# Two expert layers with attention on one core: what GpSimd does between its last scatter-add and the end of the program

## The reference, cut to what matters

```python
x = x + xattn0(layernorm(x), ctx, ctx, mask, wq, wk, wv, wo)   # 16 heads
x = x + ffn0(layernorm(x), ...)                                # 8 experts, top 2, capacity 560
x = x + xattn1(layernorm(x), ctx, ctx, mask)                   # one head, no projections
x = x + ffn1(layernorm(x), gate_w, w1, w2, w3)                 # 8 experts, top 2, no capacity
```

## Time and profile before

| what | value |
|---|---|
| device time, median of 3 runs | 1093.72 us (1085.96 to 1093.96) |
| the profiled execution's own device time | 1096.15 us |
| its span, first to last instruction of the program | 1094.3 us |
| device time outside the span | 1.85 us |
| PE busy | 953.3 us, 87% of the span |
| DVE busy | 685.4 us, 63% |
| ACT busy | 544.7 us, 50% |
| POOL busy | 479.0 us, 44% |
| end of the last instruction that counts as work (POOL, L1545) | 1080.81 us |

### The profile page before, as it was taken

The page is one execution under the profiler, slowest core; times in us unless marked ns, Lnnn a source line. Parts: engine busy times, 40 slices in busy tenths (PEclk is TensorE's granted clock), DMA queues, the critical chain, the costliest instruction groups (busy, mean ns, idle before and its releaser), DMA issues.

```text
span 1094.3 us, 23134 instructions
## 1 busy us (share of the span) xinstructions
PE 953.3 (87%) x8011; PEld 876.2 (80%) x8011; DVE 685.4 (63%) x1937; ACT 544.7 (50%) x1212; POOL 479.0 (44%) x478
## 2 busy tenths in 40 slices
PE   5899999999999478999999567854999999999994
PEld 4778788888887378998999545644999999999993
DVE  6456676576666576666666346773678778776150
ACT  3678878888888445455555223312333343343120
POOL 2023235225213346666666522474446545563222
PEclk8889999999999678999999879975999999999997
DMA  7877787878764277677766776445245434541101
GB/s 191 170 203 189 189 198 202 238 192 213 186 140 108 68 195 184 168 170 168 168 171 146 185 180 165 155 132 200 66 115 140 116 101 107 151 102 40 16 5 21
DMA packets 109670, 160.10 MB, mean 146 GB/s; under 512 B 11360, under 2 KB 98624, under 8 KB 107616
## 3 DMA queue, kind: packets, MB, share of 16 engines
q1 hardware_dynamic: 95600, 140.03, 48.5%
q0 software_dynamic: 13936, 18.33, 8.5%
HBM read 103.32 MB, written 56.96 MB: 146 GB/s over the span
## 4 chain that ended last, share of the span: by engine, by line
PE 42%; DVE 8%; POOL 5%; issue 4%; DMA 3%; ACT 1%; POOLq 0%; DVEq 0%; SPq 0%; ACTq 0%
PE ps L300 36%; DVE HTH L1293 2%; POOL x_scratch L1545 2%; PE ps L647 1%; PE ps L490 1%; DMA CN<-in_ctx_n 1%; POOL xg_scratch L1481 1%; DMA x_scratch<-YY,XG 1%; PE ps L578 1%; POOL rs L1460 1%; DVE WL L915 1%; PE ps L595 1%; POOL HTL L1533 1%; DVE st L1113 1%; ACT GT L816 1%
## 5 line engine op out<-in xcount | busy, mean ns | idle before, releaser
L300 PE MATMUL ps<-XGH,WH 128*128 128x280 f32 (+1 forms) x768 | 225.2, 293 | 9.3 <-ACT GT L816 7.1
L300 PE MATMUL ps<-XGL,WH 128*128 128x280 f32 (+1 forms) x768 | 224.5, 292 | 0.0
L300 PE MATMUL ps<-XGH,WL 128*128 128x280 f32 (+1 forms) x768 | 224.3, 292 | 0.0
L1533 POOL TENSOR_TENSOR HTL<-GT,HTH 128x280 fp32r<-128x280 f32 x128 | 132.6, 1049 | 169.4 <-DVE HTH L1293 169.4
L1165 DVE CUSTOM_DVE_ANT_0 NS<-ps,negm 112x375 f32<-112x375 f32 x256 | 138.0, 545 | 92.9 <-PE ps L406 91.9
L300 PE MATMUL ps<-WH,HTH 128*112 128x256 f32 x568 | 162.3, 286 | 1.5 <-DVE YY L1307 1.5
L300 PEld LDWEIGHTS ps<-XGH,WH 128*128 128x128 f32 x768 | 149.2, 194 | 14.1 <-ACT GT L816 10.3
L300 PE MATMUL ps<-WH,HTL 128*112 128x256 f32 x568 | 159.7, 281 | 0.0
L300 PE MATMUL ps<-WL,HTH 128*112 128x256 f32 x568 | 159.7, 281 | 0.0
L744 ACT ACTIVATE PP<-NS,MN 112x375 f32<-112x375 f32 x256 | 156.5, 612 | 3.9 <-DVE MN L1165 3.3
L300 PEld LDWEIGHTS ps<-XGH,WL 128*128 128x128 f32 x768 | 149.6, 195 | 0.0
(11 more groups left out here) (206 smaller groups left out, 1896.2 us busy)
## 6 DMA issues: line engine op xcount, KB each, us to landing
WG<-in_v SPq DMA_DIRECT2D x48, 512.0 KB, 4.1
KST<-k_scratch SPq DMA_DIRECT2D x48, 376.0 KB, 5.6
WG<-in_w SPq DMA_DIRECT2D x32, 512.0 KB, 4.3
k_scratch<-KHL SPq DMA_DIRECT2D x64, 188.0 KB
CT<-in_ctx_t SPq DMA_DIRECT2D x32, 375.0 KB, 7.1
xg_scratch<-zero SPq DMA_DIRECT2D x8, 1289.8 KB, 10.2
xg_scratch<-zero SPq DMA_DIRECT2D x16, 586.2 KB, 8.9
XG<-xg_scratch SPq DMA_DIRECT2D x14, 586.2 KB, 4.6
```

The costliest lines, as they stand in the source:

```text
L300: m = e.matmul(out_ap, l, r, start=n == 0, stop=n == len(steps) - 1)
L1533: e.tensor_tensor(HTL[:, f, cols], GT[:, gi % 3, :], HTH[:, f, cols], ALU.subtract).then_inc(hl_pool[layer], 1)
```

## The change

Two edits. The block is made with `no_gpsimd_drain=True`, and POOL's waits for the last four scatter-adds ahead of the flag's check are gone:

```diff
-        block = top.enter_context(nc.Block())
+        block = top.enter_context(nc.Block(no_gpsimd_drain=True))
...
             pool_overflow_loads(e, 0)
             pool_experts(e, 1, first_block)
-            for m in range(5 * E - NY, 5 * E):
-                e.wait_ge(*row_done(1, m))
             overflow_blocks(e, lambda j: pool_overflow(e, j))
```

## The result

The changed kernel takes 1082.67 us (median of 19 runs, 1077.58 to 1089.01) against 1092.51 us for the kernel before (19 runs, 1085.96 to 1096.9): ratio 0.991, 95% interval 0.9893 to 0.9927. That is 9.8 us; 1083.6 had been forecast, with a gain of 10.1. The profiled execution took 1085.0 us with a span of 1083.1, so 1.9 us lie outside the span, as before (1.85).

A forecast was written before the change was run, and what follows sets the result against it. PE bounds the whole (953.3 of 1094.3 us), POOL alone the end. DRAIN 6.7 plus check and jump 3.8, less 0.3 for SP and 0.1 for its new instruction, gain 10.1: 1093.72 - 10.1 = 1083.6 us; range 1076.5 to 1090.5.

The forecast's parts named there:

- The path at the end: From the last landing at 1083.6 to the span's end at 1094.3, only POOL's work sets the time.
- check and jump: POOL's flag check and branch to the end block: 3.8 us after the landing, hidden once POOL's waits go.
- The DRAIN's 6.7 us: POOL's DRAIN in the end block: all 6.7 us leave the path if nothing else takes over its work.
- The estimate beside it: End block's DRAIN: 6670 ns over 149 indirect DMAs of POOL would be 45 ns for each.
- The 181 ns at the program's start: POOL's DRAIN at the program's start, with no DMA issued yet, took 181 ns against 6.7 us at the end.
- The run-ahead of POOL's sequencer: Flag check starts at 1079.4, during the last scatter-add, putting POOL at the end block at 1083.1, before SP.
- The second rival: At the end block POOL still arrives last, at 1084.6 or 1085.7; gain 9.4 or 8.3 us; chance 0.10.
- The end block's new instruction: Each of four other engines signals with one instruction more; only SP's counts, 0.1 us (bounds 0 and 0.2).
- The rival of the work that comes back behind the span: The DRAIN's 6.7 us are paid after the program's last instruction; gain 3.4 us, time 1090.3; chance 0.25.
- The slower rival: Behind the span, 149 DMAs' entries are waited out, then cleared: 13.3 us against 10.1 won, 1096.9; chance 0.03.
- From the span to the median: The 10.1 us span gain was taken off the median, 1093.72, giving 1083.6, 0.92% faster.

The follow-up runs named there:

- the flag alone: Kernel before with only no_gpsimd_drain=True set on the block, removing POOL's end DRAIN; POOL's last four waits stay. Ratio 0.9951 (0.9928 to 0.9974).
- the waits alone: Kernel before with only POOL's waits for the last four scatter-adds removed; the end block's DRAIN stays. Ratio 0.9974 (0.9949 to 1.0).

## Why the prediction was right, point by point

**The path at the end.** Right: it was POOL's alone from the last landing on, by check and jump, DRAIN, meeting. Both edits shorten it, and from the landing on nothing else moved: SP is at its DRAIN 0.3 us behind the landing in both kernels.

**The DRAIN's 6.7 us.** Right in size and in that nothing takes it over: with the flag alone the distance fell by 6.7 us and the device time outside the span stayed at 1.8. The estimate beside it, 45 ns for each of 149, named the right thing to count and the wrong price. It is 82 ns, and the 6.67 us pay for 80 of them, not for 149; the right size at the end is a measured row and owes nothing to the estimate. One quotient can't tell a low price for all from a higher price for some. The 181 ns at the program's start weren't the price of an empty DRAIN either: POOL was still busy beside it (the DRAIN ran from 0.31 to 0.49, and POOL's last MEMSET of L1902 ended at 0.44), and an empty one took 107.

**The run-ahead of POOL's sequencer.** Right, and by more than assumed. The check was placed at the earliest just behind the start of the scatter-add, 4.2 us before the landing; it started 0.2 us before that start (1078.08 against 1078.28). So the sequencer doesn't wait for POOL to begin the scatter-add before it goes on. The jump cost in its new place what it had cost: 2.8 us from the end of POOL's branch to its DRAIN with the waits alone, as before, and 2.5 to 2.8 us in the ten kernels that have POOL's DRAIN in the end block. What it is made of, no run shows. POOL's arrival at the end block has no row of its own in this kernel; with the jump at 2.8 us, as with the waits alone, it is 1081.7 by estimate, 1.2 us ahead of SP's signal. The second rival, in which POOL arrives last, didn't come true. Its price was 0.1 us too high in the prediction, which set POOL's 1084.6 and 1085.7 against SP's DRAIN at 1083.9 and not against its signal at 1084.0: the gains would have been 9.5 and 8.4 us.

**The end block's new instruction.** 0.1 us was allowed. SP's DRAIN starts at 1082.8, its signal at 1082.9, and 0.2 us later the program is over. From the landing to the end I had 1084.2 - 1083.6 = 0.6 us, and 0.6 was measured.

**The rival of the work that comes back behind the span** had a quarter of the chance. It is out: the device time outside the span was between 1.8 and 1.95 us in every run of every kernel here, with POOL's DRAIN and without it.

**The slower rival** needed the same growth, to over 11.95 us, and is out with it. Its two walks of 6.7 us through the entries of 149 DMAs were an assumption; no run shows such a walk.

**From the span to the median.** The profiled execution gained 11.2 us of span, of which 1.1 are PE's end, at 1076.98 in place of 1078.04, which the change doesn't explain: it lies ahead of the first place where the two programs differ. The medians differ by 9.8 and the distance by 10.1; that they agree to 0.3 us is in part luck, since single runs scatter by some 3 us. That the gain lies under 1% (0.9%) was right as well. The interval excludes no change only because there are 19 runs of each; three runs that lie 8 us apart could not have shown it.

## What to carry to other kernels

When the span goes on behind the last work, read the sequencers' lines there, engine by engine, and measure from the last landing to the end: in this kernel 10.7 us of 1094 lay there, and no list of busy time named them. Here a DRAIN on GpSimd paid 82 ns for each indirect DMA issued since the last one, as far as 77 of them, so if it has to stay, put others where GpSimd idles: with them spread, the program ended 0.6 us behind its last landing. Keep only one engine's waits for outputs at the end, ahead of nothing else: without the DRAIN it is SP's waits that hold the program until its outputs have landed (they ended at 1082.5, and SP's signal, at 1082.9, was the last). A check that only has to be passed, with its jump (3.8 us together here), belongs in front of a wait for a transfer and not behind it.

## What was not expected of the hardware

- GpSimd's DRAIN costs 107 ns with nothing to clear and 82 ns more for each indirect DMA since the last DRAIN (5, 45 and 77 of them), even 3.6 us and more after all had landed. With 97 to 149 in the end block it took 6.7 to 8.2 us, in no order of their number.
- The DRAIN doesn't wait for the last landing before it begins: started 0.4 us ahead of it, it was as long as when started 3.8 us behind it. But where it had little to clear it didn't end before the landing: with 5 left, and started 1.0 us ahead of it, it took 1.3 us in place of 0.5 and ended 0.2 us behind it.
- A DRAIN's row can start while GpSimd still executes what stands ahead of it in the program: the first one in the middle started at 377.4, and three scatters ahead of it ended only by 380.0. Its length then holds that work too.
- A load into a register that stands behind an indirect DMA in the program started 0.2 us before the DMA's own execution on GpSimd (1078.08 against 1078.28).
- The run-to-run scatter of this kernel goes with TensorE's granted clock: over the 19 runs of the changed kernel the mean granted clock lay between 0.933 and 0.949, the two slowest runs (1089.01 and 1087.14 us) had 0.933 and 0.936, and the fastest (1077.58) 0.948. The order isn't strict: the highest, 0.949, went with 1080.91 us.
